# Signalling each finished group of TensorE products by a drain instead of by the group's last matmul, in the edge loop of a graph-attention kernel

## The chip, the cores and the metric

The kernel runs on one core of a Trainium2 chip. The metric is the device time of one execution in microseconds, the median of three runs. The trace is of one further execution, taken by the hardware profiler.

## The reference: what is computed

Five layers of a heterogeneous graph transformer over N = 6250 nodes of 128 features (4 heads of 32) and E = 100000 edges sorted by their destination, and at the end a layer norm of the sum with the input. One layer:

```python
k, q, v = typed_linear(x, ntype, Wk | Wq | Wv)          # a matrix for each of 3 node types
kw = typed_linear_heads(k[src], etype, att)             # a 32x32 matrix for each of 6 edge types and head
a = sum(kw * q[dst], -1) * pri[:, etype].T / sqrt(32)
w = softmax of a over the edges of one destination      # segment max, exp, segment sum
m = typed_linear_heads(v[src], etype, msg) * w
h = typed_linear(segment_sum(m, dst), ntype, Wa)
x = h * alpha + x * (1 - alpha)                          # alpha by node type
```

## The kernel before

Each layer has three phases, and all engines meet between them (`end_phase`). `project_` goes over the 49 tiles of 128 nodes, keeps q in SBUF (`qn`) and stores a table in DRAM that has, for each node and each of 6 edge types, a row of 256 numbers: the transformed k and v. `edges_` goes over the edges. `output_` goes over the tiles again and applies `Wa`.

The edges phase is what matters here. Edges stand in 832 steps of 128 edges, and four steps make a position, so there are 208 positions in a layer and 1040 in all. Eight positions make a block (26 in a layer, 130 in all), the unit of the softmax. Every engine has its own `body(q, slot, use, n)` for position q, written out for 16 slots and looped by `positions`. What the engines do in position q:

- GpSimd issues four indirect gathers (L443) of 128 table rows each into `rows[:, slot]`. The ring `rows` has 16 slots. Before it fills a slot again GpSimd waits for `s_wm`, that is, for the position 16 earlier to have been weighted, and that happens 12 positions (`LAG`) after its scores.
- TensorE has three groups of products and sometimes a fourth, in this order. `turn_onehot(q + 1)`: four transposes (L588) of the one-hot matrix of destinations into bank 0 of PSUM, signalled by `s_ohp`. The expansion of q to edges: four float products (L627, each of which runs in two passes), signalled by `s_qe`. The sums of position a = q - 12: for each of two banks a zeroing product (L642) and two sums (L643, L648), signalled by `s_agg`; they wait for `s_wm` of the same body of VectorE. Then in four slots of eight, `softmax_piece(k, n)`, k = 0 to 3: one or two small products (L598, L602, L607, or L611 and L612), signalled by `s_smp`.
- ScalarE copies the transposes to SBUF (`ohT`, L721) after `s_ohp`, and builds one-hot matrices (`ohf`, `oh`: L704 and L709). The one for the sums waits for `s_agg` (L708).
- VectorE weights the messages of position a (`wmsg`, L1025 and L1029, then `s_wm`), builds every second one-hot matrix (L945, after `s_ohp`), waits for `s_qe` and the gathers and multiplies (`prod`, L1045), waits for `s_agg` of the position before and adds the sums to `acc` in two halves (L1041), with the reduction to `score` (L1053) between them, and in four slots of eight waits for `s_smp` and does its share of the softmax (L961 to L1005).

TensorE takes its tile numbers from memory. `tiles_of` loads four of them with `values_load_multi_w_load_instructions` (L228): once ahead of the expansion and once ahead of the sums. Its sequencer then works out addresses for the moving operand of L627 and the output of L648. `hold` (L254, L255) is a wait and an increment of its own semaphore by the sequencer; it stands ahead of every softmax piece. `pe.drain()` is in use already in two places: at the end of each phase (L259) and twice in the preparation (L509).

Of the kernel before, what the change touches and what calls it, by code (L numbers as in the profile page):

```python
# [34 lines left out]
P = 128  # L35
# [23 lines left out]
AW = D + H  # L59
# [6 lines left out]
def gnn(nc, x, src, dst, etype, ntype, Wk, Wq, Wv, Wa, pri, att, msg, skip, out):  # L66
# [3 lines left out]
    with ExitStack() as ctx:  # L70
        def sb(name, shape, dt=F32):
            return ctx.enter_context(nc.sbuf_tensor(name, shape, dt))

        def sem(name):
            return ctx.enter_context(nc.semaphore(name))

        ps = ctx.enter_context(nc.psum_tensor("ps", [P, 8, 512], F32))
# [3 lines left out]
        ident = sb("ident", [P, P])  # L81
        identb = sb("identb", [P, P], BF16)
# [34 lines left out]
        qn = sb("qn", [P, TILES, D])  # L117
# [4 lines left out]
        oh = sb("oh", [P, 2, 4, P], BF16)  # L122
        ohT = sb("ohT", [P, 2, 4, P])
        ohf = sb("ohf", [P, 2, 4, P])
        prod = sb("prod", [P, 2, 4 * D])
        wmsg = sb("wmsg", [P, 2, 4, AW])
        score = sb("score", [P, 2, P])
# [56 lines left out]
        s_ohp = sem("onehot_transposed")  # L184
        s_ohT = sem("onehot_copied")
        s_qe = sem("q_expanded")
# [3 lines left out]
        s_agg = sem("summed")  # L190
        s_add = sem("accumulated")
        s_smp = sem("softmax_products")
# [5 lines left out]
        def positions(eng, body):  # L198


            for k in range(RING):
                body(k, k, 0, k // BQ)
            with eng.Fori(0, ITERS) as it:
                for k in range(RING):
                    body(it * RING + (RING + k), k, it + 1, it * 2 + (2 + k // BQ))
            for q in range(QUADS - RING, QUADS + LAG + 1):
                body(q, q % RING, q // RING, q // BQ)
# [15 lines left out]
        def at(i, n=1):  # L223
            return bass.ds(i, n)

        def tiles_of(q, engine):

            _, ts = nc.values_load_multi_w_load_instructions(  # L228
                tile_of[0:1, at(4 * q, 4)], engines=[engine], min_val=0, max_val=TILES - 1,
                skip_runtime_bounds_check_because="a step's tile counts the tiles 1..TILES-1 that began before it")  # L230
            return ts

        def is_first(v, n=1):
            return isinstance(v, int) and v < n

        def beyond(v, total=QUADS):
            return isinstance(v, int) and v >= total

        def summed(q):

            a = q - LAG
            return None if is_first(a, 0) or beyond(a) else a

        def piece(slot, n):

            k = slot % BQ
            return (None, None) if k > 3 or is_first(n) or beyond(n - 1, BLOCKS) else (k, n - 1)
# [4 lines left out]
        def hold(eng, semaphore, value):  # L252

            eng.wait_ge(semaphore, value)  # L254
            eng.sem_inc(s_held, 1)  # L255
# [50 lines left out]
        def prep_sel(kb):  # L306

            return flat[:, 1024 + kb * SP_:1024 + (kb + 1) * SP_]
# [164 lines left out]
        def _(pe):  # L473
# [4 lines left out]
                      stop=True).then_inc(s_prepe, 1)  # L478
            pe.wait_ge(s_pre, 2)
            below = wmsg[:].rearrange("p a b c -> p (a b c)")[0:TILES - 1, 0:SP_]  # L480
            for k in range(2):
                last = pe.matmul(ps[:, k, 0:SP_ // 2], ones[0:TILES - 1, :],
                                 below[:, k * (SP_ // 2):(k + 1) * (SP_ // 2)], start=True, stop=True)
            last.then_inc(s_prepe, 1)
            pe.wait_ge(s_pre, 3)
            for a, (arr, _) in enumerate(prep_arrays()):
                for k in range(2):
                    for kb in range(CB):
                        last = pe.matmul(ps[:, 2 + 2 * a + k, 0:SP_ // 2], arr[:, kb, :],
                                         prep_sel(kb)[:, k * (SP_ // 2):(k + 1) * (SP_ // 2)],  # L490
                                         start=(kb == 0), stop=(kb == CB - 1))
# [3 lines left out]
            for e in range(2):  # L495
                for k in range(2):
                    last = pe.matmul(ps[0:4, 2 * e + k, 0:SP_ // 2], pick[:, e, :],
                                     dsts[:, k * (SP_ // 2):(k + 1) * (SP_ // 2)], start=True, stop=True)
# [82 lines left out]
            def edges_(l):  # L581
                def turn_onehot(q, b, pair):
                    pe.wait_ge(s_oh[b], l * (QUADS // 2) + pair + 1)
                    if not is_first(q):
                        pe.wait_ge(s_ohT, l * QUADS + q)
                    pb = ps[:, 0, :].bitcast(BF16)
                    for j in range(4):
                        last = pe.transpose(pb[:, j * P:(j + 1) * P], oh[:, b, j, :], identb[:])  # L588
                    last.then_inc(s_ohp, 1)

                def softmax_piece(k, n, par):
                    g = l * (SM * BLOCKS) + SM * n
                    if k == 0:
                        if not is_first(n):
                            hold(pe, s_smd, g)
                        hold(pe, s_dot, l * QUADS + BQ * n + BQ)

                        pe.transpose(ps[:, 1, 0:P], score[:, par, :], ident[:]).then_inc(s_smp, 1)  # L598
                    if k == 1:
                        hold(pe, s_smd, g + 1)  # L600

                        pe.matmul(ps[0:H, 1, 0:2 * BS], same_head[:], ends[:].rearrange("p e s -> p (e s)"),  # L602
                                  start=True, stop=True).then_inc(s_smp, 1)
                    if k == 2:
                        hold(pe, s_smd, g + 2)

                        pe.matmul(ps[:, 1, 2 * BS:4 * BS], same_headT[:], carry[:].rearrange("p e s -> p (e s)"),  # L607
                                  start=True, stop=True).then_inc(s_smp, 1)
                    if k == 3:
                        hold(pe, s_sme, l * BLOCKS + n + 1)  # L610
                        pe.transpose(ps[:, 1, P:2 * P], aT[:], ident[:])  # L611
                        pe.matmul(ps[:, 1, 2 * P:2 * P + H], ones[0:H, :], fade4[:, 1, :],  # L612
                                  start=True, stop=True).then_inc(s_smp, 1)

                def body(q, slot, use, n):
                    b = slot % 2
                    if is_first(q):
                        turn_onehot(0, 0, 0)
                    if not beyond(q + 1):
                        turn_onehot(q + 1, 1 - b, use * (RING // 2) + (slot + 1) // 2)  # L620
                    if not beyond(q):
                        ts = tiles_of(q, mybir.EngineType.PE)
                        pe.wait_ge(s_ohT, l * QUADS + q + 1)
                        if not is_first(q, 2):
                            pe.wait_ge(s_dot, l * QUADS + q - 1)
                        for j in range(4):
                            last = pe.matmul(ps[:, 2 + b, j * P:(j + 1) * P], ohT[:, b, j, :],  # L627
                                             qn[:, at(ts[j]), :].rearrange("p a c -> p (a c)"),
                                             start=True, stop=True)
                        last.then_inc(s_qe, 1)  # L630
                    a = summed(q)
                    if a is not None:
                        ta = tiles_of(a, mybir.EngineType.PE)
                        pe.wait_ge(s_ohf, l * QUADS + a + 1)
                        pe.wait_ge(s_wm, l * QUADS + a + 1)
                        if not is_first(a, 2):
                            pe.wait_ge(s_add, l * QUADS + a - 1)


                        for i in range(2):  # L640
                            bank = ps[:, 4 + 2 * b + i, :]
                            pe.matmul(bank[:, AW:2 * AW], identb[:], zeros[:], start=True, stop=True)  # L642
                            pe.matmul(bank[:, 0:AW], ohf[:, b, 2 * i, :], wmsg[:, b, 2 * i, :],  # L643
                                      start=False, stop=True, skip_group_check=True)
                            on = nc.s_assert_within(
                                ta[2 * i + 1] - ta[2 * i], 0, 1,
                                skip_runtime_bounds_check_because="a step moves on by one tile at most")
                            last = pe.matmul(bank[:, at(on * AW, AW)],  # L648
                                             ohf[:, b, 2 * i + 1, :], wmsg[:, b, 2 * i + 1, :],
                                             start=False, stop=True, skip_group_check=True)  # L650
                        last.then_inc(s_agg, 1)
                    k, m = piece(slot, n)
                    if k is not None:
                        softmax_piece(k, m, 1 - slot // BQ)
                positions(pe, body)
            layers(pe, edges_, output_, project_)

# [468 lines left out]
```

## Time and profile before

| | |
|---|---|
| median of 3 runs | 7933.0 us (7932.73 to 7936.94) |
| profiled execution, from first to last instruction | 9921.5 us |
| TensorE busy with matmuls | 5554.4 us, 33354 matmuls |
| TensorE busy with weight loads | 4735.9 us |
| VectorE busy | 4643.5 us |
| ScalarE busy | 4066.5 us |
| GpSimd busy | 4557.4 us |
| mean granted TensorE clock | 0.740 |

The profiled execution's own span is 9921.5 us, and that is 25% longer than the runs without a profile. This has to be kept in mind with every share that is read from it. The engines are far from full: no one of them is busy for more than 56% of the span. A busy time counts compute instructions alone; drains, waits, register and address instructions of an engine's sequencer are not in it. A view by source line shows them for TensorE as rows of `PEldq`.

### The profile page before, as it was taken

How to read it: one execution, taken by the hardware profiler on the slowest of the kernel's cores; microseconds unless marked ns; L12 is line 12 of the kernel's file. 1: busy time of each engine (PE TensorE's matmuls, PEld its weight loads, DVE VectorE, ACT ScalarE, POOL GpSimd, SP SyncE). 2: the span in 40 equal slices, each digit the busy share in tenths (PEclk: the TensorE clock that was granted, in tenths of full speed). 3: DMA queues.
4: the chain of work that ended last, by engine and by line, in shares of the span. 5: the costliest groups of instructions: out<-in, count | busy, mean ns of one | idle time of the engine just before them, and what ended most of it. 6: DMA issues, size and time to landing. Idle time of an engine off the chain costs nothing.

```text
span 9921.5 us, 147395 instructions
## 1 busy us (share of the span) xinstructions
PE 5554.4 (56%) x33354; PEld 4735.9 (48%) x33355; DVE 4643.5 (47%) x12764; ACT 4066.5 (41%) x10084; POOL 4557.4 (46%) x4797
## 2 busy tenths in 40 slices
PE   5654545586554555955555559445454594555554
PEld 3544444464444444744444447344444573444443
DVE  5254545532555555235554552355555523555555
ACT  1244444432444444324444443344444433444442
POOL 0345555433455554335555542445555424555553
PEclk9866676797677666977666679767767796676667
DMA  2322222213222221232222213222222132222221
GB/s 69 144 62 70 70 71 70 68 70 125 69 71 72 71 72 56 100 107 72 69 72 72 69 45 124 93 69 71 70 70 71 37 140 83 73 74 73 73 76 36
DMA packets 272656, 761.00 MB, mean 77 GB/s; under 512 B 87871, under 2 KB 104356, under 8 KB 271908
## 3 DMA queue, kind: packets, MB, share of 16 engines
q0 software_dynamic: 199680, 545.53, 19.2%
q1 hardware_dynamic: 72228, 208.51, 5.4%
q14 instruction: 646, 5.29, 0.2%
q8 instruction: 102, 1.67, 0.1%
HBM read 557.87 MB, written 195.88 MB: 76 GB/s over the span
## 4 chain that ended last, share of the span: by engine, by line
PE 31%; another core or an unknown queue 25%; DVEq 16%; issue 12%; DVE 10%; POOLq 3%; ACT 2%; ACTq 1%; DMA 0%; POOL 0%; SPq 0%
PE ps L535 6%; PE ps L627 6%; DVEq L1061 5%; DVEq L1051 5%; PE ps L643 4%; PE ps L648 4%; PE ps L552 3%; POOLq L459 3%; DVEq L228 2%; PE ps L555 2%; PE ps L588 1%; PE ps L642 1%; DVE prod L1045 1%; DVE wmsg L1025 1%
## 5 line engine op out<-in xcount | busy, mean ns | idle before, releaser
L443 POOL DMA_INDIRECT rows<-table,idx_now x4160 | 3981.4, 957 | 3529.5 <-DVE wmsg L1029 1878.9
L642 PE MATMUL ps<-zeros,identb 128*128 128x132 bf16 x2080 | 555.0, 267 | 3189.9 <-DVE wmsg L1029 2780.9
L704 ACT ACTIVATE prod<-iota_n,dloc 128x128 bf16<-128x128 f32 x6240 | 1988.9, 389 | 106.0 <-issue 78.7
L642 PEld LDWEIGHTS ps<-zeros,identb 128*128 128x128 bf16 x2080 | 242.1, 116 | 3353.3 <-issue 3171.5
L1045 DVE TENSOR_TENSOR prod<-ps,rows 128x512 f32<-128x512 f32 x1040 | 715.5, 688 | 2352.6 <-remote 1820.4
L709 ACT ACTIVATE ohf<-prod,ones 128x512 f32<-128x512 bf16 x1040 | 750.5, 722 | 2326.4 <-remote 1887.0
L627 PE MATMUL ps<-qn,ohT 128*128 x8320 | 1583.6, 350 | 67.8 <-issue 62.7
L627 PEld LDWEIGHTS ps<-qn,ohT 128*128 128x128 f32 x8320 | 1407.3, 255 | 135.9 <-issue 129.7
L643 PE MATMUL ps<-wmsg,ohf 128*128 128x132 f32 x4160 | 1267.6, 398 | 0.0
L648 PE MATMUL ps<-wmsg,ohf 128*128 128x132 f32 x4160 | 1090.9, 355 | 0.0
L588 PE MATMUL ps<-identb,oh 128*128 128x128 bf16 x4160 | 531.8, 268 | 730.4 <-ACT ohT L721 358.8
L643 PEld LDWEIGHTS ps<-wmsg,ohf 128*128 128x128 f32 x4160 | 894.6, 266 | 53.6
L648 PEld LDWEIGHTS ps<-wmsg,ohf 128*128 128x128 f32 x4160 | 911.4, 268 | 0.0
L721 ACT CAST ohT<-ps 128x512 f32<-128x512 bf16 x1040 | 594.4, 572 | 768.8 <-remote 538.5
L1025 DVE TENSOR_TENSOR wmsg<-rows,weight 128x512 f32<-128x512 f32 x1040 | 720.2, 693 | 380.5 <-issue 335.5
L1041 DVE TENSOR_TENSOR acc<-acc,ps 128x264 f32 x2080 | 871.5, 419 | 18.6 <-issue 11.2
L588 PEld LDWEIGHTS ps<-identb,oh 128*128 128x128 bf16 x4160 | 353.7, 119 | 833.6 <-issue 375.0
L1053 DVE TENSOR_REDUCE score<-prod 128x16 f32<-128x512 f32 x1040 | 713.0, 686 | 77.9
L424 POOL TENSOR_TENSOR rows<-h,tmask 128x384 f32 (+1 forms) x245 | 248.8, 1016 | 1043.0 <-PE ps L518 868.5
L726 ACT ACTIVATE fade<-fade 4x4 f32<-4x4 f32 x130 | 26.6, 204 | 1174.3 <-DVEq L1009 1167.5
L424 POOL TENSOR_TENSOR rows<-acc,tmask 128x384 f32 (+1 forms) x245 | 295.0, 1204 | 412.2 <-DVE acc L926 283.4
L898 DVE TENSOR_TENSOR rows<-ps,priw 128x384 f32<-128x384 f32 x490 | 250.3, 552 | 457.0 <-PE ps L535 457.0
(162 smaller groups left out, 6391.4 us busy)
## 6 DMA issues: line engine op xcount, KB each, us to landing
table<-rows SPq DMA_DIRECT2D x245, 768.0 KB, 3.2
rows<-table,idx_now POOLq DMA_INDIRECT x4160
out<-h SPq DMA_DIRECT2D x1, 3072.0 KB
wk<-in_L_gnn_Wk SPq DMA_DIRECT2D x20, 48.0 KB
wq<-in_L_gnn_Wq SPq DMA_DIRECT2D x20, 48.0 KB
wv<-in_L_gnn_Wv SPq DMA_DIRECT2D x20, 48.0 KB
wa<-in_L_gnn_Wa SPq DMA_DIRECT2D x20, 48.0 KB
attw<-in_L_gnn_rel_att SPq DMA_DIRECT2D x20, 24.0 KB
```

The lines of the kernel that those rows point to most:

```text
L443: pool.indirect_dma_start(out=rows[:, slot, j, :], out_offset=None, in_=table, in_offset=bass.IndirectOffsetOnAxis(ap=idx_now[:, half, c:c ...
L588: last = pe.transpose(pb[:, j * P:(j + 1) * P], oh[:, b, j, :], identb[:])
L627: last = pe.matmul(ps[:, 2 + b, j * P:(j + 1) * P], ohT[:, b, j, :], qn[:, at(ts[j]), :].rearrange("p a c -> p (a c)"), start=True, stop=True)
L642: pe.matmul(bank[:, AW:2 * AW], identb[:], zeros[:], start=True, stop=True)
L643: pe.matmul(bank[:, 0:AW], ohf[:, b, 2 * i, :], wmsg[:, b, 2 * i, :], start=False, stop=True, skip_group_check=True)
L648: last = pe.matmul(bank[:, at(on * AW, AW)], ohf[:, b, 2 * i + 1, :], wmsg[:, b, 2 * i + 1, :], start=False, stop=True, skip_group_check=True)
L704: act.activation(squares[:, turn % 2, j * P:(j + 1) * P], iota_n[:], ACT.Square, bias=dloc[:, at(4 * q + j)], scale=-1.0)
L709: return act.activation(out_[:, b].rearrange("p s c -> p (s c)"), squares[:, turn % 2, :], ACT.Relu, bias=ones[:, 0:1], scale=-1.0)
L1025: dve.tensor_tensor(wmsg[:, b, :, 0:D].rearrange("p s (h c) -> p s h c", h=H), rows[:, aslot, :, D:ROW].rearrange("p s (h c) -> p s h c", ...
L1041: dve.tensor_tensor(window, window, ps[:, 4 + 2 * (1 - b) + i, 0:2 * AW], ALU.add)
L1045: dve.tensor_tensor(prod[:, 0, :].rearrange("p (s c) -> p s c", s=4), ps[:, 2 + b, :].rearrange("p (s c) -> p s c", s=4), rows[:, slot, :, ...
L1053: dve.tensor_reduce(score[:, slot // BQ, (slot % BQ) * 4 * H:(slot % BQ + 1) * 4 * H].rearrange("p (s h) -> p s h", h=H), prod[:, 0, :].re ...
```

## The change

In the edge loop, each of TensorE's groups used to put its semaphore increment on its last matmul (`last.then_inc(...)`). Now the matmuls carry none, and behind each group stands `pe.drain().then_inc(...)`: an instruction of the sequencer that ends when what was issued before it has ended, and that then carries the increment. It is in all four kinds of group, the softmax pieces too. The preparation, `project_` and `output_` are unchanged; their groups still signal by the last matmul. The number of matmuls, their operands, their order and all waits are the same.

```diff
@@ turn_onehot
                     for j in range(4):
-                        last = pe.transpose(pb[:, j * P:(j + 1) * P], oh[:, b, j, :], identb[:])
-                    last.then_inc(s_ohp, 1)
+                        pe.transpose(pb[:, j * P:(j + 1) * P], oh[:, b, j, :], identb[:])
+                    pe.drain().then_inc(s_ohp, 1)
@@ softmax_piece, k == 0 (k == 1, 2 and 3 in the same way)
-                        pe.transpose(ps[:, 1, 0:P], score[:, par, :], ident[:]).then_inc(s_smp, 1)
+                        pe.transpose(ps[:, 1, 0:P], score[:, par, :], ident[:])
+                        pe.drain().then_inc(s_smp, 1)
@@ body, expansion of q
-                            last = pe.matmul(ps[:, 2 + b, j * P:(j + 1) * P], ohT[:, b, j, :],
-                                             qn[:, at(ts[j]), :].rearrange("p a c -> p (a c)"),
-                                             start=True, stop=True)
-                        last.then_inc(s_qe, 1)
+                            pe.matmul(ps[:, 2 + b, j * P:(j + 1) * P], ohT[:, b, j, :],
+                                      qn[:, at(ts[j]), :].rearrange("p a c -> p (a c)"),
+                                      start=True, stop=True)
+                        pe.drain().then_inc(s_qe, 1)
@@ body, sums
-                            last = pe.matmul(bank[:, at(on * AW, AW)],
-                                             ohf[:, b, 2 * i + 1, :], wmsg[:, b, 2 * i + 1, :],
-                                             start=False, stop=True, skip_group_check=True)
-                        last.then_inc(s_agg, 1)
+                            pe.matmul(bank[:, at(on * AW, AW)],
+                                      ohf[:, b, 2 * i + 1, :], wmsg[:, b, 2 * i + 1, :],
+                                      start=False, stop=True, skip_group_check=True)
+                        pe.drain().then_inc(s_agg, 1)
```

## Rows read from the trace of the kernel before

**Rows 1.** Stretches of the span: one `edges_`, `output_` with `project_`, the end.

```profile
core 0: us, PE busy (x) PEld busy (x) DVE busy (x) ACT busy (x) POOL busy (x), PEclk, DMA share, GB/s
414.00:1981.00 1567.00, 772.81 (x4650) 680.43 (x4651) 772.54 (x2233) 691.17 (x1766) 803.17 (x857) 0.69 0.25 71
...
2020.00:2377.00 357.00, 312.08 (x1895) 246.95 (x1894) 107.34 (x213) 106.96 (x214) 114.64 (x105) 0.96 0.28 111
...
9760.00:9921.00 161.00, 63.20 (x441) 54.27 (x441) 75.43 (x65) 25.00 (x51) 59.24 (x49) 0.74 0.14 40
```

**Rows 2.** Waits by pair, whole span: total us, times, longest us.

```profile
PE ps L642 <- DVE wmsg L1029: 2780.9, 544, 12.5
ACT ohf L709 <- remote: 1887.0, 214, 17.5
...
DVE prod L1045 <- remote: 1820.4, 244, 29.9
...
PEld ps L627 <- issue: 129.7, 321, 0.7
```

**Rows 3.** Timeline: start us, us; VectorE and ScalarE stop together.

```profile
1444.78 0.22 PE L642 MATMUL ps<-zeros,identb 128*128 128x132 bf16 x1
...
1445.68 0.39 PE L648 MATMUL ps<-wmsg,ohf 128*128 128x132 f32 x2
...
1446.55 1.15 PE L627 MATMUL ps<-qn,ohT 128*128 x8 [0.25 <-issue]
...
1453.05 0.95 POOL L443 DMA_INDIRECT rows<-table,idx_now  x1 [0.30 <-issue]
1456.54 0.69 DVE L1045 TENSOR_TENSOR prod<-ps,rows 128x512 f32<-128x512 f32 x1 [12.13 <-remote]
1456.65 0.72 ACT L709 ACTIVATE ohf<-prod,ones 128x512 f32<-128x512 bf16 x1 [9.78 <-remote]
```

**Rows 4.** The page's costliest group: GpSimd's gathers.

```profile
L443 POOL DMA_INDIRECT rows<-table,idx_now x4160 | 3981.4, 957 | 3529.5 <-DVE wmsg L1029 1878.9
```

**Rows 5.** The chain that ended last, a part without such stops.

```profile
1422.34 0.12 DVE wmsg L1025
...
1423.36 0.29 PE ps L642
...
1425.73 0.63 PE ps L607 x2
1426.38 0.22 DVE prod L989
...
1430.03 0.29 PE ps L642
...
1433.13 0.54 PE ps L588 x4
1433.67 1.12 PE ps L627 x8
1434.79 0.08 issue
1434.88 0.23 PE ps L642
```

**Rows 6.** Source lines, narrow windows: ns min/median/max, first to last start.

```profile
L509 PEldq DRAIN  x1: 2490/2490/2490, 132.6 to 132.6; - x1
...
L627 PE MATMUL ps<-qn,ohT x7: 275/275/372, 1017.2 to 1018.0; 128*128 x7
...
L228 PEldq FUSED_REGOPS  x1: 60/60/60, 1433.0 to 1433.0; - x1
...
L634 PEldq FUSED_REGOPS  x1: 51/51/51, 1433.5 to 1433.5; - x1
...
L635 PEldq EVENT_SEMAPHORE  x1: 51/51/51, 1434.7 to 1434.7; - x1
```

**Rows 7.** Timeline: behind the drain of L509, and transposes with the expansion.

```profile
134.74 0.30 PE L508 MATMUL ps<-dloc,prod 128*128 128x26 f32 x2
...
1016.41 0.40 PE L588 MATMUL ps<-identb,oh 128*128 128x128 bf16 x4
...
1017.20 1.15 PE L627 MATMUL ps<-qn,ohT 128*128 x8 [0.40 <-issue]
```

More of the change, by code:

```diff
@@ L602, in softmax_piece @@
                         pe.matmul(ps[0:H, 1, 0:2 * BS], same_head[:], ends[:].rearrange("p e s -> p (e s)"),
-                                  start=True, stop=True).then_inc(s_smp, 1)
+                                  start=True, stop=True)
+                        pe.drain().then_inc(s_smp, 1)
                     if k == 2:
@@ L607, in softmax_piece @@
                         pe.matmul(ps[:, 1, 2 * BS:4 * BS], same_headT[:], carry[:].rearrange("p e s -> p (e s)"),
-                                  start=True, stop=True).then_inc(s_smp, 1)
+                                  start=True, stop=True)
+                        pe.drain().then_inc(s_smp, 1)
                     if k == 3:
@@ L612, in softmax_piece @@
                         pe.matmul(ps[:, 1, 2 * P:2 * P + H], ones[0:H, :], fade4[:, 1, :],
-                                  start=True, stop=True).then_inc(s_smp, 1)
+                                  start=True, stop=True)
+                        pe.drain().then_inc(s_smp, 1)
                 def body(q, slot, use, n):
@@ L626, in body @@
                         for j in range(4):
-                            last = pe.matmul(ps[:, 2 + b, j * P:(j + 1) * P], ohT[:, b, j, :],
-                                             qn[:, at(ts[j]), :].rearrange("p a c -> p (a c)"),
-                                             start=True, stop=True)
-                        last.then_inc(s_qe, 1)
+                            pe.matmul(ps[:, 2 + b, j * P:(j + 1) * P], ohT[:, b, j, :],
+                                      qn[:, at(ts[j]), :].rearrange("p a c -> p (a c)"),
+                                      start=True, stop=True)
+                        pe.drain().then_inc(s_qe, 1)
                     a = summed(q)
```

## The prediction

> **What bounds the kernel now.** I read the stretches first, to part the phases. Up to 414 us the kernel prepares and projects; between two edge phases lie 357 us, and behind the last 161 us [rows 1]. So 414 + 4 x 357 + 161 = 2003 us of the profiled span are outside the edge loop, and the change doesn't touch them. The other 7918 us are the loop. A layer of it has 772.81 us of matmuls for 208 positions, 3.72 us each or 29.7 us for a block of eight, at a mean granted clock of 0.69 [rows 1], a mixture of the two levels (1.2 and 2.4 GHz): the sums of one position take 1.29 us at the high one, from 1444.78 to 1446.07 [rows 3], and 2.37 us at the low one, from 1423.36 to 1425.73 [rows 5].
>
> The waits come next, because no engine is full. The largest of TensorE is for `wmsg`. But ScalarE and VectorE have 1887.0 and 1820.4 us of waits that end at "remote" [rows 2], which is to say at nothing that the profile can name. The timeline of such a stop shows what it is. TensorE has ended its sums by 1446.07 and its expansion by 1447.70; ScalarE's `ohf` waits only for the sums, and VectorE's `prod` for the expansion and its gathers. Both start at 1456.5 to 1456.7, after GpSimd's last gather of that run [rows 3]. The increments of finished matmuls have arrived some 9 us late, and both at once. The two engines stand still in the same stretches, so the two totals are one loss of some 1850 us, not two.
>
> Does the unprofiled run have it? The profiled span less 1850 is 8070, and the median is 7933.0. If a run without profiling had these stops too, everything else would have to take a quarter less time there (7933 - 1850 = 6083 against 8070). GpSimd speaks against that: a gather starts 0.957 + 0.30 us after the one before [rows 3, 4], so 4160 of them take 5229 us, and with the 2003 outside the loop that is 7232 already. Only 700 us are left for GpSimd to stand still, where in the profile it stands still for 1878.9 for `wmsg` alone [rows 4]. I conclude that the stops belong to the profiled execution, and set my sum against 9921.5 - 1850 = 8070, within 2% of the median. From the median, the loop has 7933 - 2003 = 5930 us, that is 45.6 us for each of 130 blocks, or 5.70 for a position.
>
> What sets those 45.6 us? Not GpSimd: its 32 gathers take 40.2 us. In a part without stops, the chain of waits goes to and fro: `wmsg` of VectorE at 1422.34, TensorE's sums and a softmax piece to 1426.36, VectorE's share to 1430.03, then TensorE again through sums, piece, transposes and expansion to the next sums at 1434.88 [rows 5]. TensorE and VectorE share the path about evenly, and TensorE is idle for 45.6 - 29.7 = 15.9 us of a block. That idle time is all the cover that the change has.
>
> **The change part by part.** Removed: an increment on the last matmul of 3640 groups (three for each of 1040 positions, four for each of 130 blocks). I cost that at nothing; the matmuls stay. Added: 3640 drains of TensorE's sequencer. What a drain itself costs is seen in the preparation: it is issued at 132.6 and takes 2.49 us, so it ends at 135.1, and the last matmul before it ends at 134.74 + 0.30 = 135.04 [rows 6, 7]. The flush is some 0.05 us, and the increment leaves about that much later than now.
>
> The price is in what stands behind. Now the sequencer runs ahead of the array; loads of tile numbers and addresses are worked out while matmuls run. A drain holds all of that back until the array is empty. In order:
>
> Behind the transposes: the sequencer needs from its first instruction of `tiles_of` to the first L627. Transposes start at 1016.41 and the expansion at 1017.20, with TensorE idle in between for 0.40 us because of "issue" [rows 7]; so this preparation takes about 0.79 us even when it overlaps the transposes. After a drain it starts when they have ended. The first matmul of a refilled array takes 372 ns and not 275, another 0.10 [rows 6]. Together 0.05 + 0.79 + 0.10 = 0.94 us. Today the gap is 0 where TensorE is backlogged [rows 5] and 0.40 where it is not; such gaps total only 129.7 us [rows 2], so I take nothing off.
>
> Behind the expansion: `tiles_of` for the sums starts at 1433.0, its last address work at 1433.5, the waits at 1434.7 and L642 at 1434.88 [rows 5, 6]. The hole between 1433.5 and 1434.7 is the queue; without it I put 0.5 + 0.1 + 0.2 = 0.8, with flush and refill 0.95 us. This hides wherever the sums wait for `wmsg` anyway.
>
> Behind the sums: an address and a wait, the like of two instructions of 0.1 us pitch, with flush 0.25 us. Behind a piece, or between sums and a piece (its `hold`), 0.4 us.
>
> Per position 0.94 + 0.95 + 0.25 = 2.14, and 4 x 0.4 per block: 8 x 2.14 + 1.6 = 18.7 us a block. Added to 29.7 that makes TensorE occupied for 48.4 us, more than the 45.6 that the block lasts: TensorE becomes the bound, by 2.8 us a block at least. It won't be perfectly packed. Around the first and the third piece, sums to sums take 1430.03 - 1423.36 = 6.67 us through VectorE [rows 5], and this chain itself grows by about 0.5 (flush, `hold`, refill, flush); where VectorE's share is short, TensorE is the later. Of 15.9 us of idle time I let 3.5 remain as idle. Block: 48.4 + 3.5 = 51.9, or 6.3 more, and 130 x 6.3 = 820 us. Forecast 7933 + 820, rounded 8760 us.
>
> Bounds of the added cost: 0, if every drain falls into idle time; 130 x 18.7 = 2430 us, if none does. The 15.9 us of idle time against 18.7 of cost exclude the first if the 2.14 are right, and the gap to `wmsg` excludes the second.
>
> The Trainium skill's "TensorE: Matmul & The Clock Gate", section "Step-by-step: what each phase is for", says that TensorE's queue pulls weight loads ahead of running matmuls and that the sequencer pops the next instruction without waiting for the array to empty. The trace agrees (expansion behind transposes without a gap [rows 5]), and a drain gives up both. The same page, in "The cost: per-tile semaphore tail", says that matmuls complete in program order, so that one increment on the last is sound: by it nothing is won in correctness or time by the drain.
>
> **The rivals.**
> *The idle time swallows most of it.* For it: TensorE waits most of all for `wmsg` [rows 2], and the 0.95 us ahead of the sums lies before exactly that wait. If both preparations hide and only what stands between sums, piece and VectorE counts (4 x 0.5) with one run of TensorE in each block like that from 1433.13 to 1434.88 (0.5), a block grows by 2.5: 8260 us. Against it: occupied time above the block's length.
> *The clock falls.* With gaps behind each group TensorE is a smaller share of the time busy. All of it at the low level would take 3.72 x 2.37/1.96 = 4.5 us a position, where 1.96 is the mean of 2.37 and 1.29 at a clock of 0.69; 8 x 0.78 = 6.2 us a block or 810 us more, 9570. For it: 0.69 with gaps against 0.96 in the dense phases [rows 1]. Against it: it is low already in most of the loop.
> *The other side: late increments are real in unprofiled runs too, and a drain's comes in time.* The change is then faster once the stops that it ends exceed the 820 us that it costs, which is 44% of the 1850. All of them: 7933 - 1850 + 820 = 6903, but the gathers don't let it below 7232. I give 7400. Against it: the GpSimd count above.
> *No effect.* The sequencer doesn't hold back, or the drain is folded away: 7933. Against it: the 2.49 us in which the drain of L509 did wait [rows 6].
>
> **How the numbers follow.** Forecast (8260 halfway up to 9160): 0.60, alone 8350 to 9150. Swallowed, 8000 to 8300: 0.17. Clock, above 9160: 0.12. Other side: 0.06. No effect: 0.05. The range from 8150 to 9350 leaves out the last two, half of the clock's upper part and some of the swallowed case. Slower by over 0.2% (16 us, about what three runs can tell from no change): 0.60 + 0.17 + 0.12 = 0.89; within 0.2% 0.05; faster 0.06.
>
> **What the profile after would show.** Right: some 3640 `PEldq DRAIN` rows in the loop, L627 and L642 preceded by "issue" idle time of about 0.9 us, matmul busy time of the loop near 3.7 us a position, less idle time of L642 for `wmsg` beside it, VectorE waiting more for L627. The profiled span itself can go either way: if the sequencer's increments are not held up as the matmuls' are, the "remote" waits vanish from it and it falls while the median rises. Wrong: drains of which the next group starts within 0.2 us (then the cost is swallowed), or a clock well off 0.69.

## The result

| | median us | runs |
|---|---|---|
| before | 7934.97 | 4 (7932.73 to 7936.99) |
| changed | 9990.33 | 4 (9989.92 to 9992.82) |

The ratio is 1.2588, with a 95% interval from 1.2573 to 1.2604: 2055 us slower. The prediction was 8760 us. The direction was right, and the size was not: 827 us were expected, 2055 came.

In some sessions TensorE's signals arrive late in every execution, timed or profiled, and the kernel before then takes about 9820 us (the profile ahead of the prediction looks like one of these, and e13 to e19 are from one), so each comparison below is with a kernel before that ran beside it.

The profile after, in an ordinary session. Its page:

```profile
span 9991.0 us, 151035 instructions
...
L631 PE MATMUL ps<-qn,ohT 128*128 x8320 | 2154.6, 441 | 919.4 <-ACT ohT L725 726.5
```

Its span is that of the timed runs. The 919.4 us of idle time before the expansion are put down to ScalarE's copy `ohT` (L725), because that ended last; but the copy that ends there is of the next position's transposes, and this expansion needs the one before it. The waits of the weight loads, below, name the cause. The same stretch as in [rows 1]:

```profile
414.00:1981.00 1567.00, 1080.33 (x4658) 870.28 (x4659) 782.93 (x2238) 703.78 (x1767) 794.09 (x857) 0.50 0.25 71
```

Almost the same number of matmuls (4658 against 4650) takes 1080.33 us and not 772.81, and the column PEclk says why: 0.50 and not 0.69. TensorE is at its low level (1.2 GHz) through the whole loop. A position has 5.19 us of matmuls, where it had 3.72.

The waits by pair (total us, times, longest us), which answer to [rows 2]:

```profile
ACT ohf L713 <- PEq L655: 2385.2, 730, 4.7
...
DVE prod L1049 <- PEq L634: 2033.9, 830, 4.1
...
PEld ps L631 <- issue: 1191.5, 1040, 1.3
PEld ps L646 <- issue: 1178.0, 1039, 3.6
```

"PEq L655" and "PEq L634" are the drains of the sums and the expansion, and the waits that ended at "remote" are gone. Before each expansion (1040 times) and before the sums (1039 times) the weight load is preceded by "issue": the sequencer was preparing. In [rows 2] that wait stood at 129.7 us for the expansion.

The timeline of TensorE for one position of the plain kind:

```profile
1467.89 0.61 PE L588 MATMUL ps<-identb,oh 128*128 128x128 bf16 x4 [0.26 <-issue]
1469.40 2.07 PE L631 MATMUL ps<-qn,ohT 128*128 x8 [0.91 <-ACT ohT L725]
1472.09 0.27 PE L646 MATMUL ps<-zeros,identb 128*128 128x132 bf16 x1 [0.61 <-issue]
...
1473.79 0.65 PE L652 MATMUL ps<-wmsg,ohf 128*128 128x132 f32 x2
1474.85 0.60 PE L588 MATMUL ps<-identb,oh 128*128 128x128 bf16 x4 [0.41 <-issue]
```

From transposes to transposes it is 6.96 us: 5.03 of matmuls and idle times of 0.91, 0.61 and 0.41 us behind the three drains. The drains are what was expected of them. The view by source line (ns min/median/max) has one behind each expansion; it begins some 0.4 us after its group and ends with it (in the position above it is issued at 1469.8 and lasts 1.69 us, and the expansion ends at 1469.40 + 2.07 = 1471.47):

```profile
L634 PEldq DRAIN  x1040: 1519/1690/1700, 418.5 to 9777.0; - x174
```

### The profile page after: what moved, and what is told of

Its sections match the earlier page's. It is cut to its first block, busy times and chain, and to the rows that moved or that the text cites. A ratio compares the mean times of both kernels' runs of the same rounds, so it can differ in the third digit from the quotient of the medians.

```text
span 9991.0 us, 151035 instructions
## 1 busy us (share of the span) xinstructions
PE 7123.2 (71%) x33354; PEld 5713.6 (57%) x33355; DVE 4678.3 (47%) x12764; ACT 4125.0 (41%) x10084; POOL 4520.7 (45%) x4797
## 4 chain that ended last, share of the span: by engine, by line
PEld 31%; issue 20%; PEldq 19%; PE 13%; ACT 6%; DVE 4%; POOLq 3%; POOL 2%; ACTq 1%; DVEq 1%; DMA 1%; SPq 0%
PEld ps L631 12%; PEld ps L647 8%; PEld ps L652 7%; PE ps L535 6%; PEldq L228 4%; ACT ohT L725 4%; PEldq L589 3%; PE ps L552 3%; PEldq L655 3%; POOLq L459 3%; POOL rows L443 2%; PEldq L634 2%; PE ps L555 2%; PEld ps L588 1%; PEld ps L646 1%
## 5 line engine op out<-in xcount | busy, mean ns | idle before, releaser
L631 PE MATMUL ps<-qn,ohT 128*128 x8320 | 2154.6, 441 | 919.4 <-ACT ohT L725 726.5
L631 PEld LDWEIGHTS ps<-qn,ohT 128*128 128x128 f32 x8320 | 1853.3, 328 | 1191.5 <-issue 1191.5
L647 PE MATMUL ps<-wmsg,ohf 128*128 128x132 f32 x4160 | 1558.8, 478 | 0.0
L652 PE MATMUL ps<-wmsg,ohf 128*128 128x132 f32 x4160 | 1345.7, 427 | 0.0
L646 PE MATMUL ps<-zeros,identb 128*128 128x132 bf16 x2080 | 621.8, 299 | 891.0 <-issue 751.4
L652 PEld LDWEIGHTS ps<-wmsg,ohf 128*128 128x128 f32 x4160 | 1157.5, 337 | 0.0
L647 PEld LDWEIGHTS ps<-wmsg,ohf 128*128 128x128 f32 x4160 | 1104.9, 326 | 72.6
L588 PE MATMUL ps<-identb,oh 128*128 128x128 bf16 x4160 | 628.8, 306 | 449.5 <-issue 347.2
L646 PEld LDWEIGHTS ps<-zeros,identb 128*128 128x128 bf16 x2080 | 264.9, 127 | 1179.5 <-issue 1178.0
L725 ACT CAST ohT<-ps 128x512 f32<-128x512 bf16 x1040 | 605.7, 582 | 685.3 <-PEq L589 571.2
```

The costliest lines, as they stand in the source:

```text
L652: pe.matmul(bank[:, at(on * AW, AW)], ohf[:, b, 2 * i + 1, :], wmsg[:, b, 2 * i + 1, :], start=False, stop=True, skip_group_check=True)
L725: act.copy(ohT[:, b].rearrange("p s c -> p (s c)"), ps[:, 0, :].bitcast(BF16)[:, 0:4 * P]).then_inc(s_ohT, 1)
```

## The experiments

**One kind of drain at a time (e1, e2, e3).** Each is the kernel before with one line of the change:

```diff
-                    last.then_inc(s_ohp, 1)          # e1; e2 has s_qe, e3 has s_agg
+                    pe.drain().then_inc(s_ohp, 1)
```

> Only the group of transposes is signalled by a drain; all else as before. Theory P (each drain exposes the sequencer's preparation of the next group on TensorE, and the longer idle gaps let the granted clock fall): 0.91 us more of TensorE per position, but a block has 15.9 us in which TensorE is idle, so part is hidden: 150 to 500 us more than before, clock below 0.69 in the loop. Rival F (a drain has a fixed price, 2057 us over 3640 drains, 0.565 us each, wherever it stands): 1040 x 0.565 = 588 us more.

> Only the expansion of q is signalled by a drain. Theory P: 0.62 us of preparation per position, and it lies ahead of the wait for wmsg, where TensorE is idle anyway: 0 to 300 us more than before. Rival F: 588 us more.

> Only the sums are signalled by a drain. Theory P: 0.3 to 0.4 us per position between the sums and the next group: 50 to 350 us more. Rival F: 588 us more. The three single edits together: P expects less than 1200 us, F 1764 us.

Measured beside 7933.6 us: e1 7924.6 (0.9989, 0.9979 to 0.9999), e2 7937.1 (1.0006, 0.9996 to 1.0015), e3 7982.9 (1.0065, 1.0048 to 1.0082). Together 44 us of the 2055. A fixed price per drain is out; so is my own size for e1. Nine of the ten executions of e1 lie between 7918.5 and 7927.3 us, with a mean clock of 0.782 to 0.790; the tenth took 9109.8 us at a mean clock of 0.536. It has no trace, so nothing is built on it, but it warns against calling a single drain safe. The waits and the stretch of e1 show the cover:

```profile
POOL rows L443 <- issue: 1612.8, 3896, 4.8
PEld ps L627 <- issue: 1133.5, 1035, 1.3
```

```profile
414.00:1500.00 1086.00, 722.13 (x4377) 616.32 (x4377) 733.68 (x2110) 647.23 (x1661) 764.78 (x812) 0.73 0.34 97
```

The preparation ahead of the expansion is exposed in full (1133.5 us over 1035 positions) and costs nothing, at a clock of 0.73. GpSimd's gathers wait hardly for any other engine (80.4 us in all for `wmsg`); their idle time is "issue". The timeline of GpSimd at the start of a block shows where it goes:

```profile
1028.58 0.95 POOL L443 DMA_INDIRECT rows<-table,idx_now  x1 [0.30 <-issue]
1029.53 0.22 POOL L439 COPY idx_now<-idx 128x32 int32 x1
1033.45 0.97 POOL L443 DMA_INDIRECT rows<-table,idx_now  x1 [3.70 <-issue]
```

Gathers are 1.25 us apart, and around the copy of the block's indices and its drain 4.87 us. So GpSimd needs 31 x 1.25 + 4.87 = 43.6 us of the 45.6 of a block. That makes it the engine that sets the pace; e8, below, tests this.

**The drain without the increment (e4).**

```diff
                     last.then_inc(s_ohp, 1)          # and so for all four kinds
+                    pe.drain()
```

> All 3640 drains are there, but the increments are back on the last matmul of each group; a drain stands bare behind it. Theory P: the hold-back of the sequencer is what costs, so the time is that of the changed kernel within 1% (9890 to 10090 us). Rival I (the increment itself travels later or slower from a drain than from a matmul, and the engines behind it wait for that): clearly faster than the changed kernel, by 0.1 us or more for each increment on the path, that is over 300 us.

Measured 9942.0 us (1.2535, 1.2514 to 1.2556), clock 0.50 in the loop. Who carries the increment is worth 48 us (the interval of the changed kernel begins at 1.2573); what a drain holds back costs the rest, by itself or through the clock, which the next experiment parts.

**Products in the idle time (e5), and the same in the kernel before (e12).** All drains, and work for the array where it stands idle:

```diff
+                def filler(bank, n):
+                    pe.matmul(ps[:, bank, 0:n], ident[:], alpha[:].rearrange("p l t -> p (l t)")[:, 0:n],
+                              start=True, stop=True)
...
+                        filler(2 + b, 240)           # ahead of tiles_of(q) and the expansion
...
+                        filler(4 + 2 * b, 160)       # ahead of tiles_of(a) and the sums
```

The wait for the reader of that bank moves ahead of it.

> The changed kernel with 2080 products more, whose results nobody reads: one of 240 float columns behind the drain of the transposes, into the bank that the expansion overwrites next, and one of 160 behind the drain of the expansion, into the bank of the sums. They lie where the array stands idle while the sequencer prepares (0.91 and 0.62 us). Theory C (most of the 2057 us is the clock: with idle gaps behind each group it stays at its low level through the whole loop, 0.50, so 3.7 us of matmuls per position became 5.2): the clock rises above 0.70 in the loop and the time falls to 8000 to 8900 us though the kernel does more. Rival S (the hold-back alone costs, the clock follows from it and gives nothing back): 9990 us or more.

> The kernel before with the two idle-time products and nothing else: the control of e5. Theory G and C: GpSimd sets the pace whatever the clock is, so the clock rises above 0.80 in the loop and the time stays within 0.5% of before. Rival (these products speed up any kernel like this one, so that e5 says nothing of the drains): several per cent faster than before.

Measured: e5 7982.1 us beside 7944.5 (1.0044, 1.0030 to 1.0058); e12 7933.5 beside 7934.7 (0.9999, 0.9990 to 1.0009). With 2080 float products more, the changed kernel gets back 2008 of the 2055 us that it had lost. The same products do nothing for the kernel before, although they raise its clock too (the mean of an execution goes from 0.817 to 0.863). The stretch and the timeline of e5, and the stretch of e12:

```profile
414.00:1500.00 1086.00, 829.64 (x5079) 598.64 (x5079) 724.84 (x2075) 653.51 (x1652) 767.04 (x801) 0.95 0.33 95
```

```profile
1007.03 0.67 PE L583 MATMUL ps<-alpha,ident 128*128 128x240 f32 x2 [0.21 <-issue]
1007.78 1.15 PE L636 MATMUL ps<-qn,ohT 128*128 x8
1009.20 0.53 PE L583 MATMUL ps<-alpha,ident 128*128 128x160 f32 x2 [0.27 <-issue]
1009.95 0.22 PE L652 MATMUL ps<-zeros,identb 128*128 128x132 bf16 x1 [0.21 <-issue]
```

```profile
414.00:1500.00 1086.00, 777.10 (x5129) 671.15 (x5130) 731.73 (x2100) 646.77 (x1657) 765.00 (x810) 0.84 0.34 96
```

The expansion takes 1.15 us where the changed kernel needs 2.07, and the clock of e5's stretch is 0.95. Of the clock of the kernel before in an ordinary session only the mean of an execution is known, 0.817; it was not profiled in one.

**Tile numbers loaded ahead of the transposes (e6).**

```diff
                     b = slot % 2
+                    if not beyond(q):
+                        ts = tiles_of(q, mybir.EngineType.PE)
+                    a = summed(q)
+                    if a is not None:
+                        ta = tiles_of(a, mybir.EngineType.PE)
```

> The changed kernel with both loads of tile numbers moved ahead of the transposes, so that no drain stands before them; all 3640 drains stay. Theory C with exposure: the idle time ahead of the expansion falls from 0.91 to about 0.35 us and ahead of the sums from 0.62 to about 0.2, a position of 6.95 us becomes 6.0 or less, 9000 us at the low clock and 8000 to 8900 if the clock recovers. Rival F (a fixed price for each drain): 9990 us.

Measured 9610.6 us (1.2094, 1.2074 to 1.2115). The waits say why it is so little:

```profile
PE ps L588 <- issue: 1297.9, 1000, 1.9
```

The loads were not taken out of a drain's shadow but moved into another's: the drain of the sums holds them back, and the transposes wait 1.3 us for the sequencer. The stretch from 414 to 1500 has a clock of 0.55.

**Two kinds of drain (e7).** The lines of e1 and e2 together.

> Drains behind the transposes and behind the expansion; sums and softmax pieces signal by the last matmul. Each of the two alone cost nothing (0.9989 and 1.0006). Theory C: the two together take about 1.5 us a position and 12 us a block, near the idle time that TensorE has at its mixed clock, so this is close to the point where the clock falls: either under 8100 us with the clock above 0.70 in the loop, or over 9300 us at 0.50, and little between. Rival (costs simply add, less the cover): 8300 to 8900 us at a clock between.

Measured 9159.1 us (1.1511, 1.1480 to 1.1543). Alone the two cost -9 and +4 us, together 1215. The stretch:

```profile
414.00:1500.00 1086.00, 788.88 (x3536) 663.86 (x3537) 594.05 (x1699) 526.57 (x1347) 627.99 (x673) 0.50 0.28 80
```

The clock is at its low level as in the changed kernel. A position takes (9159 - 2003)/1040 = 6.88 us. The time lies a little under what I gave for a fallen clock.

**GpSimd's pause taken away (e8), and the same with all drains (e9).** The next block's indices are copied three positions ahead:

```diff
-                    if slot % BQ == 0:
-                        pool.tensor_copy(idx_now[:, half, :], idx[:, at(4 * q, BS)])
-                        pool.drain()
+                    if is_first(q):
+                        pool.tensor_copy(idx_now[:, 0, :], idx[:, 0:BS])
+                        pool.drain()
+                    elif slot % BQ == 0:
+                        hold(pool, s_idx, l * (BLOCKS - 1) + n)
+                    if slot % BQ == 5 and not beyond(q + 3):
+                        if is_first(q, RING) and half == 1:
+                            for k in range(BQ):
+                                hold(pool, s_gath[k], l * (QUADS // RING) * 64 + 64)
+                        pool.tensor_copy(idx_now[:, 1 - half, :], idx[:, at(4 * q + 12, BS)]).then_inc(s_idx, 1)
```

(The innermost `hold` makes the second copy of a layer wait for the gathers that still read the indices it overwrites.)

> The kernel before, TensorE untouched. GpSimd copies the next block's indices three positions ahead and signals it by a semaphore, in place of a copy and a drain at the block's start (which leave 3.58 us between two gathers there). Theory G (GpSimd's gathers set the pace of the kernel before, 32 x 1.25 + 3.6 us a block, and that is why single drains on TensorE are free): up to 130 x 3.4 = 440 us less, 7500 to 7800 us. Rival T (TensorE and VectorE set it, as the prediction said): within 0.5% of 7934 us.

> The changed kernel (all drains) with GpSimd's indices prepared ahead. In the changed kernel TensorE sets the pace at 61.4 us a block, GpSimd needs 40 to 44. Theory: nothing is gained, 9900 to 10050 us, clock 0.50 in the loop. Rival (GpSimd's pace is part of the changed kernel's time too): 440 us less, 9550.

Measured: e8 7491.0 us (0.9434, 0.9419 to 0.9450); e9 9975.1 (1.2576, 1.2555 to 1.2597). Without the drains GpSimd's pause is worth 454 us beside 7944.5, 3.5 a block; with them nothing that can be told from zero (9975.1 against 9990.3 in another session; the intervals 1.2555 to 1.2597 and 1.2573 to 1.2604 overlap). In e8 the longest wait of this kind, 4.8 us in e1, is 0.9 us:

```profile
POOL rows L451 <- issue: 1147.4, 3808, 0.9
```

This settles that GpSimd sets the pace of the kernel before and not that of the changed one, and e8 is faster than both.

**Products and prepared indices (e10 with all drains, e11 without).**

> All drains, the two idle-time products, and GpSimd's indices ahead. Theory C: with the clock kept high TensorE needs about 2.9 us of its own matmuls and 2 us of preparation a position, 40 to 43 us a block with the pieces, so the time follows GpSimd down: 7500 to 7800 us. Rival (at the high clock the drains' hold-back already fills TensorE, and e5 was bound by it): 7950 us or more.

> No drains, the two idle-time products, and GpSimd's indices ahead. GpSimd alone gave 7491 us, 5488 of it in the loop, 42.2 us a block against 40.0 for 32 gathers without a pause. What is left above GpSimd's pace is waits of a mixed clock (0.80 in the loop). Theory: a higher clock takes some of it, 7300 to 7480 us. Rival (products in the way of real work cost more than the clock gives): above 7500 us.

Measured: e10 7832.8 us (0.9878, 0.9858 to 0.9899), e11 7503.4 (0.9459, 0.9443 to 0.9474). Against e8, the products give nothing (e11): my expectation of a gain there was wrong. And e10 stays 329 us above e11 and misses my range by 33. Once GpSimd is faster, the drains cost something even at a high clock (0.94 in the loop): 0.32 us a position, which I take for hold-back that GpSimd's pause had covered; no run parts it further.

**The kernel before again (e13).**

> The kernel before, unchanged, profiled once more. Expected: the time of before; a profiled span equal to it within 0.2%, no waits that end at 'remote', GpSimd's gathers 1.25 us apart with one longer gap of 3.6 us a block, a clock of 0.74 to 0.80 in the loop. If instead the profiled span is near 9921 us again, profiling this kernel is what makes the difference.

Measured 9826.6 us (median of eight executions, 9821.9 to 9839.1), and a profiled span of 9824.0:

```profile
ACT ohf L709 <- remote: 1969.4, 174, 17.4
DVE prod L1045 <- remote: 1921.9, 280, 27.8
ACT ohT L721 <- remote: 394.9, 61, 28.8
```

The profiler doesn't make the stops of [rows 3]: the timed executions of this series are as long as the profiled one, 1893 us above 7934. What brings such a session about stays open. `ohf` and `ohT` wait for TensorE alone, so it is TensorE's signals that come late there; `prod` waits for gathers too, and the pages of e13 and of the trace of before have no time to landing for the gathers, where that of e1 has 2.8 us, so for `prod` the two can't be told apart.

**The changed kernel, the same with 8 columns, 240 and 160, and one product, side by side (e14, e16 to e19).**

> As e5, with 8 columns in place of 240 and 160: the same instructions and the same order of waits, but hardly any time on the array. Theory C (it is the array's busy time that keeps the clock up): the clock stays at 0.50 in the loop and the time at 9900 to 10150 us. Rival (the moved waits or the presence of an instruction behind the drain did it): about 7980 us as e5.

> The changed kernel again, beside the three that follow. If the kernel before takes 7935 us here: 9990 us, clock 0.50 in the loop. If it takes 9827: TensorE's signals come late for drains too (e14 showed waits for them of up to 30 us), about 11000 us.

> 8 columns in place of 240 and 160. Theory C (the array's busy time keeps the clock up): as e16 within 1.5%, clock 0.50 in the loop. Rival (the moved waits or an instruction behind the drain): as e18.

> As e5: 240 and 160 columns. Theory C: clock above 0.9 in the loop and over 15% less time than e16 and e17.

> The product of 240 columns behind the transposes alone; the sums' part is as in the changed kernel. Theory C: a clock and a time between e16 and e18. It says whether one filled gap is enough.

Measured, with the clock from 414 to 1500 us (all in the session with late signals; the products of 8 columns were never run in an ordinary one):

| | us | ratio to before (about 9820) | clock |
|---|---|---|---|
| e14, 8 columns | 11136.6 | 1.1332 (1.1307 to 1.1357) | 0.50 |
| e16, the changed kernel | 11153.9 | 1.1351 (1.1326 to 1.1375) | 0.50 |
| e17, 8 columns | 11124.9 | 1.1321 (1.1294 to 1.1348) | 0.50 |
| e19, 240 columns behind the transposes | 10840.1 | 1.1044 (1.1001 to 1.1088) | 0.57 |
| e18, 240 and 160 columns | 10394.8 | 1.0578 (1.0548 to 1.0609) | 0.75 |

e17 has the instructions and the order of waits of e18 and differs only in the width of the products; its time is that of the changed kernel. So neither a product's presence nor the moved waits hold the clock up: wide products do, and one wide product a position (e19) does less than two. The stretches of e17 and e18, and TensorE in e17:

```profile
414.00:1500.00 1086.00, 772.15 (x3230) 630.78 (x3230) 464.34 (x1323) 417.00 (x1049) 492.11 (x530) 0.50 0.22 63
```

```profile
414.00:1500.00 1086.00, 666.14 (x3459) 504.42 (x3460) 496.71 (x1417) 445.67 (x1124) 532.60 (x567) 0.75 0.24 68
```

```profile
1004.82 0.59 PE L583 MATMUL ps<-alpha,ident 128*128 128x8 f32 x2 [0.21 <-issue]
1005.54 2.07 PE L636 MATMUL ps<-qn,ohT 128*128 x8
1007.88 0.59 PE L583 MATMUL ps<-alpha,ident 128*128 128x8 f32 x2 [0.27 <-issue]
```

These lines hold a warning. By the profile e17's idle times are 0.21 and 0.27 us, the same as in e5, and TensorE is busy for 772 us against 666 in e18 (in part because the same work lasts longer at the low clock); yet its clock is 0.50. A product of 8 columns is shown as 0.59 us (x2), nearly as long as one of 240 at the high clock (0.67 in e5). Idle and busy time read from the profile don't tell the clock; the same place filled with wide products or narrow ones does.

e18 gains 6.8% over e16, not the 15% that I expected, and its clock is 0.75 and not above 0.9: signals come late here for drains as well, and that part the clock can't give back. In e16 it is the drain itself that lasts long, up to 21.2 us, where no drain of the expansion lasted over 1.70 in the ordinary session:

```profile
DVE prod L1049 <- PEq L634: 3151.8, 808, 30.1
L634 PEldq DRAIN  x1040: 1515/1690/21155, 419.6 to 10947.7; - x174
```

The longest wait of this kind was 4.1 us in the ordinary session.

## Why the prediction was wrong

**The sums of the drain itself were near.** Flush, preparation and refill were put at 0.94, 0.95 and 0.25 us behind the three groups; the timeline has 0.91, 0.61 and 0.41, together 1.93 against 2.14. Only the first was right by itself; the errors of the other two partly cancel. The idle time that would remain was put at 3.5 us a block. With measured numbers: 8 x 5.19 = 41.5 us of matmuls, 8 x 1.93 = 15.4, and 4 x 0.18 for the pieces (0.33 and 0.26 in place of 0.41) make 57.7; the block takes (9990 - 2003)/130 = 61.4, so 3.7 remain. With the base wrong by so much, that the 3.5 came out is partly luck.

**The step that failed is the clock.** The sum took matmuls at 29.7 us a block, "at a mean granted clock of 0.69", and added the idle times to them as if the clock didn't depend on these. It fell to 0.50 for the whole loop, and the matmuls grew to 41.5 us. This is the term that was mis-sized, by 11.8 us a block or 1534 us, which is more than the miss of 1230. The idle times go the other way: 16.2 us a block and not 18.7, some 330 us less. The base itself was of the other kind of session: the timed runs of the kernel before have a mean clock of 0.817, its profile 0.740. The rival "the clock falls" was there, at 0.12. Its price of 4.5 us a position was too low as well (5.19 measured), probably, though no run shows it, because part of the low clock behind the 0.69 lay in stops without matmuls; its 9570 is still short of the result. Clock and idle time can't be added, as e5 shows: at the high clock the drains cost 0.44%. At the high level a position has 2.84 us of matmuls (1.29 [rows 3], 0.40 [rows 7], 1.15) and 1.93 of idle time, 4.8 us, which is under GpSimd's pace of 43.6/8 = 5.5. At the low level 5.03 + 1.93 = 6.96 is over it. So the same idle time is covered or not by the clock, and what TensorE does in it decides the clock (e5, and e17 against e18). Which level a kernel ends at is read from the runs and not derived: each drain alone leaves the clock of the stretch at 0.73 or 0.74 and is nearly free (e1 to e3), two together bring it to 0.50 and cost 15% (e7), though at the low level e1 would be over the pace too (5.03 + 0.91 = 5.94).

**"Not GpSimd: its 32 gathers take 40.2 us" was the second error.** It left out the pause at the block's start, 3.6 us. e8 shows that GpSimd set the pace, so the cover was not "15.9 us of idle time" of an engine on the path but of one beside it. I read the total of 1878.9 us for `wmsg`, which e1, in a session without stops, has at 80.4. The pause stood in the next row of GpSimd's waits of before: 3720 gathers at 0.30 us make 1116 of its 1650.6 us, and the longest wait is 4.0 us:

```profile
POOL rows L443 <- issue: 1650.6, 3720, 4.0
```

**"The stops belong to the profiled execution" was right for the sum and wrong as a statement.** Taking them off gave 8070 for 7933. But e13 finds timed executions that are as long as the profiled one. The profile after has no such stops because its session had none, not because drains escape them (e16).

**The other rivals.** No effect, and a gain by signals in time: neither happened; in a session with late signals the change still costs 13.5%. Swallowed idle time is what a single drain shows.

The Trainium skill's "TensorE: Matmul & The Clock Gate", section "A second HAM failure mode: psum-queue depth-cycling", says that short idle times between groups of matmuls can throw the clock back and forth between its levels. Here it doesn't come back at all: 0.50 over the stretch from 414 to 1981 us, with idle times of 0.41 to 0.91 us between groups.

## What to carry to other kernels

Don't add idle time to matmul time at the clock of before: work the sum out at both levels, and compare each with the next engine's pace; if one level is under it and the other over, single edits may look free and a pair of them may not. A drain on TensorE is cheap itself and dear by what its sequencer prepares behind it, so keep the increment on the last matmul. Where TensorE must stand idle for preparation, a wide product that nobody reads can be worth a fifth of the run (one of 8 columns did nothing), but first look for the pause of the engine that sets the pace: here it was a copy and a drain on GpSimd, worth 5.7%.

## What was not expected of the hardware

The clock of a stretch was raised from 0.50 to 0.95 by 2080 products without use, and the time fell from 9990 to 7982 us (e5). Narrow products in the same places, which fill the same idle time by the profile, left it at 0.50 (e17). And the same kernel takes 7935 or 9827 us from session to session (e13), with waits of up to 28.8 us for increments of TensorE's matmuls (`ohT`), and drains that last up to 21.2 us (e16); what brings this about stays open.
